# A four-layer transformer kernel with fused expert FFNs: the order of its steps planned by a clock per engine, and the low halves of the weights made by GpSimd

## The chip, the cores and the metric

One NeuronCore of one Trainium2 chip. The metric is the time of one execution on the device in microseconds; the kernel before has a median of 562.09 us in 3 runs.

## The reference

Four layers, all in float32, on `x` of 4 batches x 512 tokens x 128 channels; each layer adds its result to `x`, and reads a layernorm of it:

```python
x = x + attn_a(layernorm(x))    # channel attention, 8 heads of 16 channels, over 512 tokens
x = x + ffn(layernorm(x))       # 8 experts of 336 hidden units, router softmax, actor picks how many
x = x + attn_b(layernorm(x))    # S = q k^T * scale; S *= piecewise factor of sigmoid(S); softmax
x = x + ffn(layernorm(x))       # the same weights again
# ffn: scores = probs where rank(probs) < argmax(actor_logits) + 1
#      out += scores[e] * (silu(h @ gate[e].T) * (h @ up[e].T)) @ down[e].T
```

## The kernel before

The work is cut into steps, each for one batch of 512 tokens. A is the first attention (steps stats, xn, ag, xT, ar, asim, ass, ascale, asT, amax, aexp, awo, am, am2, y), F an FFN (stats, xn, xT, xl, route, rexp, inner, rsum, rrank, tanh, gelu, act, actk, sbc, yT), B the second attention (stats, xn, xT, xl, bqk, bqkl, bs, bsp, bexp, bv, bpT, bo, byx). The F batches 0 to 3 are the first FFN layer, 4 to 7 the second: eight in all.

The FFN's hidden units of all experts stand in 21 chunks (CH) of 128, so there are 168 chunks, numbered k over all eight batches. A chunk is six TensorE passes `gu` (line 1039): gate and up, each as high x high, high x low and low x high in the 4-byte float32r type (`three`, lines 923 to 927); ScalarE's silu of gate into `sl` (616); VectorE's product of up and `sl` into `t2` (`uk`, line 859); GpSimd's product of that with the router's scores `sbc` (`um`, line 513); and the down product into the accumulator bank 7 (line 1061, in float32, two passes). Gate of chunk k waits for silu of k-2, up for the `uk` of k-2. There are 16 buffers `t2`, so gate of chunk k may not be ahead of down of chunk k-16. `um` of a batch needs its `sbc`, so no down product starts before the router chain of its batch (route to sbc) is through.

The weights come from HBM in 21 pieces of 128x384 (192 KB): piece j is gate's (j % 3 = 0), up's (1) or down's (2) of three chunks. ScalarE copies a piece of gate or up to its high half (line 587), VectorE subtracts that from the staged piece to make the low half, WGl or WUl (line 743). Both are parts of the step `wp`, or of `wph` and `wpl` for the first two pieces. TensorE waits before chunks 0, 3, 6, ..., 18 for the low halves of the next three chunks (line 1043).

Every engine runs its part of one list of steps in the order of the list, and waits on semaphores; so the order of the list is the order on each engine. The list comes from `plan()` (line 155). After a written-out PRELUDE it adds for each k the steps `gu` and `uk`, then up to two `um` and `down`, then from each thread (one for each batch of F, A, B, with a start and due offsets in chunks: F_STEPS, A_STEPS, B_STEPS, B_STARTS) the steps that are due at k, and one weight piece at most. A step is put off by one chunk at most if ScalarE's or VectorE's costs of this k exceed TensorE's (COST, DEBT). What was put off in an earlier chunk is otherwise not looked at. B batch 3 starts near chunk 91 and ends with byx behind chunk 131; F batch 7 starts at 132, its sbc stands behind chunk 150.

Matmul results of all steps but the chunks use three PSUM banks in turn (TURNS).

Of the kernel before, what the change touches and what calls it, by code (L numbers as in the profile page):

```python
# [29 lines left out]
F32 = mybir.dt.float32  # L30
# [18 lines left out]
AFTER_POOL = 1.6  # L49
# [42 lines left out]
F_STEPS = [(0, "stats"), (1, "xn"), (3, "xT"), (4, "xl"), (6, "route"), (7, "rexp"), (7, "inner", 0),
           (10, "inner", 1), (9, "rsum"), (12, "rrank"), (12, "tanh"), (12, "gelu"), (14, "act"),
           (14, "actk"), (18, "sbc")]
A_STARTS = (9, 25)
B_STARTS = (25, 48, 67, 90)
M_START = 7
SHIFTS = 1
F_AHEAD = 22


# [7 lines left out]
POOL_COST = dict(um=1.35, stats=1.4, ass=.8, bqkl=1.4, actk=1.1, inner=1)  # L109
COST = dict(stats=(0, 0, 1.2), xn=(0, 0, 1.1), xT=(.4, .5, 0), xl=(0, 0, .6), ag=(.9, .3, 0), ar=(.5, .4, .4),  # L110
            asim=(.7, 0, 0), ass=(0, 0, .1), ascale=(0, 0, .3), asT=(.1, 0, 0), amax=(0, 0, .5), aexp=(0, 3, 0),
            awo=(0, 0, .5), am=(.3, .3, 0), am2=(.3, .3, 0), y=(.9, 0, .6), route=(2, 1.1, .3), rexp=(0, 2.7, 0),
            rsum=(0, 0, 1.3), rrank=(0, 0, 1.1), tanh=(0, .5, 0), gelu=(0, 0, .6), act=(.9, 0, 0), actk=(0, 0, 1.3),
            sbc=(.4, .5, 0), yT=(.4, 0, .6), bqk=(.7, 1, 0), bs=(.7, .5, 0), bsp=(0, 0, .9),
            bv=(.7, 0, .6), bexp=(0, 1.2, 0), bpT=(.4, .5, 0), bo=(.9, .1, 0),
            byx=(0, 0, 1.4))
DEBT = 0.1


def thread(kind, b, steps, start):  # L120

    norm = ("stats", "xn", "xT", "xl")
    return [start, [(s[0], (s[1], kind, b) if s[1] in norm else (s[1], b) + s[2:])
                    for s in steps], 0]


def needs(s):


    kind, b = s[0], s[-1] if s[0] in ("stats", "xn", "xT", "xl") else s[1]  # L130
    prev = b - 1
    if kind == "stats":
        return {"A": [], "F": [("y", b) if b < NB else ("byx", b - NB)], "B": [("yT", b)]}[s[1]]
    if kind == "xT" and s[1] == "A":
        return [("y", b - 2), ("ag", b)]
    if kind == "am2" and b == 0:
        return [("wv", 0)]
    if kind in ("xT", "xl") and s[1] == "B":
        return [("bv", prev)]
    if kind == "bo":  # L140
        return [("bpT", b, i) for i in range(NT)]
    if kind == "yT":
        return [("down", CH * (b + 1) - 1)]
    if kind == "bexp":
        return [("byx", prev), ("bsp", b, s[-1], 3)]
    if kind == "bpT":
        return [("byx", prev)] + [("bexp", b, i) for i in range(NT)]
    return {"ag": [("ar", prev)], "ar": [("asim", prev)], "ass": [("ascale", prev)],
            "ascale": [("asT", prev), ("amax", prev)], "amax": [("aexp", prev)], "aexp": [("am", prev)], "awo": [("am", prev)],
            "am": [("am2", prev)], "am2": [("y", prev)],  # L150
            "bqk": [("bs", prev, NT - 1)], "bs": [("bpT", prev, NT - 1)], "bv": [("byx", prev)],
            "route": [("act", prev)], "rsum": [("actk", prev)], "actk": [("sbc", prev)]}.get(kind, [])


def plan():

    last = CH * 2 * NB
    threads = [thread("F", n, F_STEPS, CH * n - F_AHEAD) if n else thread("F", 0, F0_STEPS, 0) for n in range(2 * NB)]  # L160
    threads += [[CH * (n + 1) + 3, [(0, ("yT", n))], 0] for n in range(2 * NB - 1)]
    threads += [[M_START, [(0, ("wbT", 0)), (2, ("wvp", 0)), (4, ("bvp", 0))], 0]]
    threads += [thread("B", b, B_STEPS, B_STARTS[b]) for b in range(NB)]
    threads += [thread("A", 1, A1_STEPS, 0)] + [thread("A", b, A_STEPS, A_STARTS[b - 2]) for b in range(2, NB)]
    pieces = [("wp", j) for j in range(2, NPIECES)]
    steps, done, order = [], set(), {}
    free_after = []
    debt = [0.0, 0.0]
    pool_free = [0.0]
    um_end, downs = [], [0]  # L170

    def ready(s):
        if not all(v in done or v[1] < 0 for v in needs(s)):
            return False
        if s[0] == "xn" and order[s[1:]] >= 2:
            two_before = [v for v, i in order.items() if i == order[s[1:]] - 2][0]
            if ("xT",) + two_before not in done:
                return False
        if s[0] == "stats" and len(order) >= 2:
            two_before = [v for v, i in order.items() if i == len(order) - 2][0]  # L180
            if ("xn",) + two_before not in done:
                return False
        n = 0 if s[0] == "bo" and s[2] else TURNS.get(s[0], 0)
        return all(len(free_after) + i < 3 or free_after[len(free_after) + i - 3] in done for i in range(n))

    def add(s):
        steps.append(s)
        done.add(s)
        if s[0] in POOL_COST:
            pool_free[0] = max(pool_free[0], k) + POOL_COST[s[0]] / 2.25  # L190
# [12 lines left out]
    def products(k, most):  # L203

        for _ in range(most):
            j = len(um_end)
            if ("uk", j) in done and ("sbc", j // CH) in done and pool_free[0] < k + 1:
                add(("um", j))
                um_end.append(pool_free[0])
            if downs[0] < len(um_end) and um_end[downs[0]] + AFTER_POOL <= k:  # L210
                add(("down", downs[0]))
                downs[0] += 1

    k = -1
    for s in PRELUDE:
        assert ready(s), s
        add(s)
    while k < last - 1:
        if (k + 1) % CH or ("xl", "F", (k + 1) // CH) in done:
            k += 1  # L220
            add(("gu", k))
            assert k < NT2 or ("down", k - NT2) in done
            add(("uk", k))
        else:
            for th in threads:
                th[0] -= th[0] <= k
        products(k, 2)
        pe = 2.2
        act, dve = debt[0] + 0.6, debt[1] + 0.7
        for th in threads:  # L230
            while th[1] and th[0] + th[1][0][0] <= k:
# [5 lines left out]
                if not ready(s) or late:  # L237
                    th[0] += 1
                    th[2] += 1
                    break  # L240
# [936 lines left out]
```

## Time and profile before

| | |
|---|---|
| runs | 560.51, 562.09, 563.34 us; median 562.09 |
| profiled execution | 562.99 us, span 561.2 us, mean granted TensorE clock 0.963 |
| TensorE (PE) busy | 508.4 us, 91% |
| VectorE (DVE) busy | 368.8 us, 66% |
| GpSimd (POOL) busy | 279.2 us, 50% |
| ScalarE (ACT) busy | 239.4 us, 43% |

PE, PEld (its weight loads), DVE, ACT and POOL are the engines' names in the rows. "Busy" counts running instructions; a matmul's end is modelled, so a busy PE can still have short gaps. The granted clock is the share of TensorE's full speed; a stretch at half has 0.5.

### The profile page before, as it was taken

How to read it: one execution, taken by the hardware profiler on the slowest of the kernel's cores; microseconds unless marked ns; L12 is line 12 of the kernel's file. 1: busy time of each engine (PE TensorE's matmuls, PEld its weight loads, DVE VectorE, ACT ScalarE, POOL GpSimd, SP SyncE). 2: the span in 40 equal slices, each digit the busy share in tenths (PEclk: the TensorE clock that was granted, in tenths of full speed). 3: DMA queues.
4: the chain of work that ended last, by engine and by line, in shares of the span. 5: the costliest groups of instructions: out<-in, count | busy, mean ns of one | idle time of the engine just before them, and what ended most of it. 6: DMA issues, size and time to landing. Idle time of an engine off the chain costs nothing. (4 is left out here: it accounts for less than half of the span.)

```text
span 561.2 us, 6465 instructions
## 1 busy us (share of the span) xinstructions
PE 508.4 (91%) x2134; PEld 359.3 (64%) x2134; DVE 368.8 (66%) x781; ACT 239.4 (43%) x399; POOL 279.2 (50%) x268
## 2 busy tenths in 40 slices
PE   7776487999897988999998999979999999999997
PEld 6754364667564764677655677656776576667664
DVE  3646737366649789678989279894797946274221
ACT  3355232444372264732654424744337452433221
POOL 4111516722875239554465434554455455464753
PEclk9979779999998999899998899998999999999999
DMA  8500000000000000000000000000000000000000
GB/s 254 169 1 1 1 0 2 0 0 1 1 2 0 1 0 1 1 0 2 1 1 0 1 0 2 0 0 2 19 2 0 1 19 1 1 2 19 1 0 19
DMA packets 7917, 7.38 MB, mean 13 GB/s; under 512 B 716, under 2 KB 7756, under 8 KB 7884
## 3 DMA queue, kind: packets, MB, share of 16 engines
q1 hardware_dynamic: 7884, 6.97, 4.0%
q8 instruction: 17, 0.28, 0.2%
q14 instruction: 16, 0.13, 0.1%
HBM read 5.91 MB, written 1.05 MB: 12 GB/s over the span
## 5 line engine op out<-in xcount | busy, mean ns | idle before, releaser
L513 POOL TENSOR_TENSOR t<-t,sbc 128x512 f32<-128x512 f32 x168 | 217.5, 1314 | 126.8 <-DVE t L859 98.3
L859 DVE TENSOR_TENSOR t<-bank,sl 128x512 f32<-128x512 f32 x168 | 114.5, 685 | 134.1 <-PE bank L927 106.0
L616 ACT ACTIVATE sl<-bank 128x512 f32<-128x512 f32 x168 | 100.0, 597 | 181.1 <-PE bank L927 163.5
L1061 PE MATMUL bank<-t,WD 128*128 128x512 f32 x336 | 168.2, 603 | 0.0
L925 PE MATMUL bank<-xhF,WGh 128*128 128x512 f32 x168 | 99.6, 593 | 22.4 <-DVE WUl L743 21.2
L1061 PEld LDWEIGHTS bank<-t,WD 128*128 128x128 f32 x336 | 64.7, 192 | 32.6 <-issue 19.8
L925 PE MATMUL bank<-xhF,WUh 128*128 128x512 f32 x168 | 69.1, 411 | 4.1 <-DVE t L859 4.1
L927 PE MATMUL bank<-xhF,WUl 128*128 128x512 f32 x168 | 68.5, 408 | 0.0
L926 PE MATMUL bank<-xlF,WUh 128*128 128x512 f32 x168 | 68.5, 407 | 0.0
L927 PE MATMUL bank<-xhF,WGl 128*128 128x512 f32 x168 | 68.0, 405 | 0.0
L926 PE MATMUL bank<-xlF,WGh 128*128 128x512 f32 x168 | 67.8, 403 | 0.0
L925 PEld LDWEIGHTS bank<-xhF,WGh 128*128 128x128 f32 x168 | 33.0, 196 | 42.6 <-DVE WUl L743 22.8
L718 DVE TENSOR_SCALAR xn<-X,mv,rstd 128x128 f32<-128x128 f32 x64 | 40.3, 691 | 8.8 <-POOL rstd L481 8.8
L926 PEld LDWEIGHTS bank<-xlF,WGh 128*128 128x128 f32 x168 | 33.1, 197 | 17.1 <-issue 15.1
L925 PEld LDWEIGHTS bank<-xhF,WUh 128*128 128x128 f32 x168 | 32.5, 194 | 13.7 <-DVE t L859 6.2
L480 POOL TENSOR_SCALAR rt<-mv 128x4 f32<-128x4 f32 x16 | 3.5, 221 | 73.8 <-DVE mv L707 73.5
L927 PEld LDWEIGHTS bank<-xhF,WUl 128*128 128x128 f32 x168 | 32.7, 195 | 8.3
L927 PEld LDWEIGHTS bank<-xhF,WGl 128*128 128x128 f32 x168 | 32.7, 194 | 7.9
L926 PEld LDWEIGHTS bank<-xlF,WUh 128*128 128x128 f32 x168 | 32.8, 195 | 7.5
L616 ACT ACT_TABLE_LOAD x20 | 25.7, 1283 | 0.4
L500 POOL TENSOR_TENSOR sx<-rk,pr 128x512 f32<-128x512 f32 x8 | 8.4, 1054 | 32.3 <-DVE rk L850 32.3
L646 ACT ACTIVATE Sb<-bank 128x512 f32<-128x512 f32 x16 | 9.6, 599 | 17.7 <-PE bank L927 17.5
(176 smaller groups left out, 683.6 us busy)
## 6 DMA issues: line engine op xcount, KB each, us to landing
stage<-in_gate SPq DMA_DIRECT2D x7, 192.0 KB, 5.3
stage<-in_up SPq DMA_DIRECT2D x7, 192.0 KB, 5.6
WD<-in_down SPq DMA_DIRECT2D x7, 192.0 KB, 5.6
X<-in_x SPq DMA_DIRECT2D x4, 256.0 KB, 5.2
out<-X SPq DMA_DIRECT2D x4, 256.0 KB, 2.3
raw<-in_small SPq DMA_DIRECT2D x1, 388.0 KB, 4.4
raw<-in_small SPq DMA_DIRECT2D x1, 192.0 KB, 2.7
rows<-in_row SPq DMA_DIRECT2D x1, 136.0 KB
```

Source lines behind the costliest of these rows:

```text
L480: chain(pool.tensor_scalar(rt[:, :], mv[:, :, 1], by, more, ALU.mult, ALU.add))
L500: pool.tensor_tensor(sx[:, :, :, :], rk[:, :, :].unsqueeze(3).to_broadcast([P, NT, E, P // E]), pr[:, :, :].unsqueeze(3).to_broadcast([P, ...
L513: pool.tensor_tensor(t2[k % NT2][:, :], t2[k % NT2][:, :], sbc[k // CH % 2][:, :], ALU.mult).then_inc(a_done, 1)
L616: act.activation(sl[k % NSL][:, :], bank[k % 2][:, :], ACT.Silu).then_inc(silu_done, 1)
L646: act.activation(Sb[:, i, :], m_bank(t)[:, :], ACT.Copy).then_inc(n_free(t), 1)
L718: r = dve.tensor_scalar(xn[:, i, :], X[:, NT * q + i, :], mv[:, i, 0:1], rstd[:, i:i + 1], ALU.subtract, ALU.mult)
L859: dve.tensor_tensor(t2[k % NT2][:, :], bank[2 + k % 2][:, :], sl[k % NSL][:, :], ALU.mult).then_inc(t2_done, 1)
L925: pe.matmul(out, lh, rh, start=start, stop=False)
L926: pe.matmul(out, lh, rl, start=False, stop=False)
L927: return pe.matmul(out, ll, rh, start=False, stop=stop)
L1061: pe.matmul(OACC[:, :], WD[:, c, :], t2[k % NT2][:, :], start=(c == 0), stop=(c == CH - 1))\
```

## The change

`plan()` is written anew. It holds a clock for each engine, `t`; STAGES gives for each step the engines it passes through and the time on each; `add` moves the clocks and notes when a step is finished (`fin`). Steps that begin on another engine than TensorE enter when their input is finished and their engine isn't ahead of TensorE by more than DVE_AHEAD, ACT_AHEAD or POOL_AHEAD. Of the steps that begin on TensorE the first ready one in the order of deadlines enters (`threads`, whose first number is the deadline in chunks); then a down product, if its input is finished; else the next chunk; else TensorE's clock goes on by 0.1. `gu` is now two steps, `gate` and `up`, and ScalarE's copy of the accumulator (line 622) is a step of its own, `yc`. Pieces 3 to 20 of the weights (12 of gate and up) have their low half made by GpSimd; two of them are in the prelude.

```diff
-F_AHEAD = 22
+STAGES = dict(
+    stats=(("dve", 1.35), ("pool", 1.5)), xn=(("dve", 1.9),), xT=(("pe", .45), ("act", .6)), xl=(("dve", .7),),
...
+    bexp=(("exp", .85),), bv=(("pe", 1.35), ("dve", .7)), bpT=(("pe", .45), ("act", .6)), bo=(("pe", .9),),
+    byx=(("dve", 2.2),), wp=(("act", .5), ("pool", 1.15)), wph=(("act", .5),), wpl=(("dve", .6),),
...
+TABLE = 1.3
+HOP = 0.1
+PE_MARGIN, BANK_MARGIN = 0.5, 0.3
+DVE_AHEAD, ACT_AHEAD, POOL_AHEAD = 2.6, 1.6, 1.5
+A_FROM = (0, 0, 6, 26)
+F_AHEAD = 24
...
+    threads = [(0, 0, [("wp", j) for j in range(5, NPIECES) if j % 3 != 2])]
+    threads += [(CH * n - 4, CH * n - F_AHEAD, thread("F", n, f_kinds)) for n in range(2 * NB)]
+    threads += [(CH * n - 14, A_FROM[n], thread("A", n, a_kinds)) for n in range(1, NB)]
+    threads += [(CH * (n + 1) + 4, 0, [("yc", n), ("yT", n)]) for n in range(2 * NB - 1)]
+    threads += [(40, 6, [("wbT", 0), ("wvp", 0), ("bvp", 0)])]
+    threads += [(CH * (NB + b) - 12, 0, thread("B", b, b_kinds)) for b in range(NB)]
+    threads.sort(key=lambda th: th[0])
...
+                    if begins <= gus and at <= now + 0.2 and banks_free(s) <= now \
+                            and max(t[e], at) + min(cost, 1.6) <= now + ahead[e]:
+                        add(s)
...
+                if begins <= gus and ready_at(s) + PE_MARGIN <= now and banks_free(s) + BANK_MARGIN <= now:
+                    best = best or (s, th)
...
+        down_at = fin["um", downs] + PE_MARGIN if downs < ums else 1e9
+        if down_at <= now:
+            add(("down", downs))
+            downs += 1
+        elif can_gu and (gu_at <= now + 1.5 or gu_at <= down_at):
+            add(("gate", gus))
+            add(("up", gus))
+            add(("uk", gus))
+            gus += 1
...
+                if kind == "wp":
+                    j = s[1]
+                    pool.wait_ge(wh_ready, 2 * (j // 3) + j % 3 + 1)
+                    hi, lo = piece_of(j)
+                    pool.tensor_tensor(lo, stage[j][:, :], hi.bitcast(F32), ALU.subtract).then_inc(wl_pool, 1)
...
-                if kind in ("wp", "wpl") and s[1] % 3 != 2:
+                if kind == "wpl":
...
-                        pe.wait_ge(wl_dve, 2 * (c // WCH) + 2)
+                        pe.wait_ge(wl_pool if c else wl_dve, 2 * (c // WCH) if c else 2)
```

In these lists of order a row is one instruction of the engine: its place, its line, what it writes and reads; lines of the changed kernel are 62 to 71 higher.

GpSimd, from the norms of the prelude to batch 0's router chain. Before (hq is the router chain's gelu input, sx what sbc is transposed from, t the buffers t2):

```order
40 L480 TENSOR_SCALAR rt_82<-mv_78 128x4
41 L481 TENSOR_TENSOR rstd_80<-rt_82,nhalf 128x4
42 L504 TENSOR_SCALAR hq<-hq 50x512
43 L507 TENSOR_TENSOR hq<-hq,xa 50x512
44 L489 TENSOR_TENSOR rs<-ss,nhalf 128x2
45 L500 TENSOR_TENSOR sx<-rk,pr 128x512
```

The changed kernel, the same place:

```order
43 L574 TENSOR_TENSOR WUl<-stage_141,WUh 128x384
44 L574 TENSOR_TENSOR WGl<-stage_142,WGh 128x384
45 L574 TENSOR_TENSOR WUl<-stage_143,WUh 128x384
46 L551 TENSOR_TENSOR rs<-ss,nhalf 128x2
47 L574 TENSOR_TENSOR WGl<-stage_144,WGh 128x384
48 L574 TENSOR_TENSOR WUl<-stage_145,WUh 128x384
49 L566 TENSOR_SCALAR hq<-hq 50x512
50 L569 TENSOR_TENSOR hq<-hq,xa 50x512
51 L574 TENSOR_TENSOR WGl<-stage_146,WGh 128x384
```

Six weight rests stand ahead of the router chain's first instruction, six behind it, and all twelve ahead of sx.

VectorE, before the actor product of batch 4, which waits for gelu (`hq<-hq,xa`). Before:

```order
356 L859 TENSOR_TENSOR t_118<-bank,sl_102 128x512
357 L824 TENSOR_TENSOR ge<-ge,tri 128x256
358 L826 TENSOR_TENSOR gt<-gt,ge 128x256
359 L827 TENSOR_REDUCE rk<-gt 128x32
360 L832 SCALAR_TENSOR_TENSOR hq<-hq,xa 50x512
361 L893 TENSOR_TENSOR mk_160<-mk_160,mk_162 128x512
```

The changed kernel:

```order
324 L887 TENSOR_TENSOR ge<-pr 128x256
325 L926 TENSOR_TENSOR t_115<-bank,sl_103 128x512
326 L926 TENSOR_TENSOR t_116<-bank,sl_102 128x512
327 L899 SCALAR_TENSOR_TENSOR hq<-hq,xa 50x512
328 L891 TENSOR_TENSOR ge<-ge,tri 128x256
329 L893 TENSOR_TENSOR gt<-gt,ge 128x256
330 L894 TENSOR_REDUCE rk<-gt 128x32
```

The three instructions of rrank have gone behind gelu, and the score instructions on mk that stood among them are elsewhere.

VectorE, where the last B batch ends (byx writes bt and X) and batch 7's norm begins. Before:

```order
558 L908 SCALAR_TENSOR_TENSOR bt<-bank,bri,rows 128x128 x4
559 L912 TENSOR_TENSOR X<-X,bt 128x512
560 L859 TENSOR_TENSOR t_108<-bank,sl_102 128x512
561 L704 BN_STATS bst<-X 128x6 x4
562 L707 BN_AGGR mv_79<-bst 128x2 x4
563 L859 TENSOR_TENSOR t_109<-bank,sl_103 128x512
564 L718 TENSOR_SCALAR xn_76<-X,mv_79,rstd_81 128x128 x4
565 L859 TENSOR_TENSOR t_110<-bank,sl_102 128x512
566 L859 TENSOR_TENSOR t_111<-bank,sl_103 128x512
567 L859 TENSOR_TENSOR t_112<-bank,sl_102 128x512
568 L738 TENSOR_TENSOR xlF_74<-bank,xhF_72 128x512
```

The changed kernel:

```order
560 L975 SCALAR_TENSOR_TENSOR bt<-bank,bri,rows 128x128 x4
561 L979 TENSOR_TENSOR X<-X,bt 128x512
562 L926 TENSOR_TENSOR t_106<-bank,sl_102 128x512
563 L771 BN_STATS bst<-X 128x6 x4
564 L774 BN_AGGR mv_79<-bst 128x2 x4
565 L785 TENSOR_SCALAR xn_76<-X,mv_79,rstd_81 128x128 x4
566 L864 TENSOR_TENSOR X<-bank,X 128x512
567 L805 TENSOR_TENSOR xlF_74<-bank,xhF_72 128x512
568 L926 TENSOR_TENSOR t_107<-bank,sl_103 128x512
```

Before, four products of chunks stand between the norm's first instruction and xlF; now none does: t_106 is chunk 146's and t_107 chunk 147's, which needs xlF. In the changed list batch 7's sbc stands behind chunk 160, with the down product of chunk 147 next. ScalarE's list has 54 table loads (ACT_TABLE_LOAD) instead of 40.

## Rows read from the trace of the kernel before

**Rows 1.** Windows: length; busy us (instructions) of PE, PEld, DVE, ACT, POOL; clock; DMA.
```profile
25.70:94.60 68.90, 46.59 (x186) 34.93 (x186) 40.32 (x87) 28.16 (x52) 22.88 (x21) 0.85 0.00 1
94.60:141.50 46.90, 46.21 (x204) 32.98 (x204) 25.99 (x79) 21.30 (x35) 17.92 (x19) 1.00 0.00 1
141.50:448.40 306.90, 287.68 (x1188) 199.82 (x1188) 242.77 (x456) 145.48 (x233) 168.21 (x140) 0.97 0.01 2
448.40:505.40 57.00, 57.00 (x249) 40.40 (x247) 29.80 (x60) 22.77 (x38) 32.40 (x29) 1.00 0.02 5
```
**Rows 2.** The chain that ended last, near the end: start us, us, what.
```profile
539.50 0.86 PE bank L1061 x2
...
541.75 0.86 PE bank L1061 x2
```
**Rows 3.** Waits of TensorE: waiter <- releaser, us in total, times, longest us.
```profile
PE bank L925 <- DVE WUl L743: 21.2, 6, 7.8
PE bank L945 <- DVE xn L718: 5.3, 5, 2.6
...
PE bank L925 <- DVE xlS L738: 2.9, 1, 2.9
```
**Rows 4.** Timeline from 61 us: start us, us, engine, line, operation.
```profile
61.93 0.53 DVE L743 TENSOR_TENSOR WGl<-stage,WGh 128x384 fp32r<-128x384 f32 x1
...
63.57 8.93 POOL L513 TENSOR_TENSOR t<-t,sbc 128x512 f32<-128x512 f32 x7
63.70 4.87 DVE L718 TENSOR_SCALAR xn<-X,mv,rstd 128x128 f32<-128x128 f32 x4 [0.46 <-POOL rstd L481]
68.50 1.63 DVE L743 TENSOR_TENSOR WUl<-stage,WUh 128x384 fp32r<-128x384 f32 x1
```
**Rows 5.** The chain that ended last, 367 to 379 us.
```profile
367.55 1.51 DVE ge L820
...
370.25 1.47 DVE mk L884
371.72 0.35 DVE mk L885
...
376.25 0.70 DVE hq L832
...
376.99 1.87 PE bank L1029 x8
```
**Rows 6.** Groups by line: busy us, mean ns of one, then idle before.
```profile
L1112 PE MATMUL bank<-v,PT 128*128 128x128 f32 x128 | 15.6, 275 | 0.0
```
**Rows 7.** Groups by line: the low halves on VectorE, the same subtraction on GpSimd.
```profile
L494 POOL TENSOR_TENSOR ql<-qF,qh 128x512 fp32r<-128x512 f32 x4 | 5.6, 1395 | 2.0 <-ACT qh L639 2.0
...
L743 DVE TENSOR_TENSOR WUl<-stage,WUh 128x384 fp32r<-128x384 f32 x7 | 5.4, 775 | 1.9 <-ACT WUh L587 1.8
...
L743 DVE TENSOR_TENSOR WGl<-stage,WGh 128x384 fp32r<-128x384 f32 x7 | 4.0, 574 | 2.2 <-ACT WGh L587 2.2
```
**Rows 8.** Groups by line: GpSimd's products, a table load, the copy of sbc.
```profile
L513 POOL TENSOR_TENSOR t<-t,sbc 128x512 f32<-128x512 f32 x168 | 217.5, 1314 | 126.8 <-DVE t L859 98.3 <-ACT sbc L610 28.1
...
L616 ACT ACT_TABLE_LOAD x20 | 25.7, 1283 | 0.4
...
L610 ACT ACTIVATE sbc<-bank 128x512 f32<-128x512 f32 x8 | 4.8, 597 | 5.0 <-PE bank L1037 5.0
```
**Rows 9.** Timelines of VectorE: batch 0's norm, and byx of B batch 3.
```profile
19.58 0.87 DVE L704 BATCH_NORM_STATS2 bst<-X 128x6 f32<-128x128 f32 x4
...
20.78 1.08 DVE L718 TENSOR_SCALAR xn<-X,mv,rstd 128x128 f32<-128x128 f32 x4
...
24.84 0.69 DVE L738 TENSOR_TENSOR xlF<-bank,xhF 128x512 fp32r<-128x512 f32 x1 [1.38 <-ACT xhF L537]
...
466.14 1.12 DVE L908 SCALAR_TENSOR_TENSOR bt<-bank,bri,rows 128x128 f32<-128x128 f32 x4 [1.09 <-PE bank L1112]
```
**Rows 10.** Groups by line: one of the eight instructions of a score block.
```profile
L884 DVE TENSOR_SCALAR mk<-Sb 128x512 bf16<-128x512 f32 x16 | 11.4, 713 | 6.7 <-ACT Sb L646 6.7
```

More of the change, by code:

```diff
@@ L107 @@
 FREED_BY = dict(asim="ascale", asT="amax", act="actk")
[L109 to L124, printed above, removed]
-def needs(s):
[L130 to L134, printed above, removed]
-        return [("y", b - 2), ("ag", b)]
[L136 to L152, printed above, removed]
@@ L165, in plan @@
-    pieces = [("wp", j) for j in range(2, NPIECES)]
-    steps, done, order = [], set(), {}
-    free_after = []
[L168 to L184, printed above, removed]
+    steps, fin, order = [], {}, {}
@@ L186, in add @@
+    free_after = []
+    t = dict(pe=0.0, act=0.0, dve=0.0, pool=0.0)
+    table = ["exp"]
+    pe_end = {}
     def add(s):
         steps.append(s)
-        done.add(s)
-        if s[0] in POOL_COST:
-            pool_free[0] = max(pool_free[0], k) + POOL_COST[s[0]] / 2.25
+        at = max([fin[v] for v in inputs(s) if v in fin], default=0.0)
+        if s[0] in ("gate", "up"):
+            at = 0.0
+        for e, cost in STAGES[s[0]]:
+            if e in ("exp", "silu"):
+                cost += TABLE * (table[0] != e)
+                table[0] = e
+                e = "act"
+            if s[0] in ("gate", "up") and e == "pe":
+                at = max([fin[v] for v in chunk_inputs(s)], default=0.0)
+            at = max(at + HOP, t[e]) + cost
+            t[e] = at
+            if e == "pe":
+                pe_end[s] = at
+        fin[s] = at
@@ L201, in add, with chunk_inputs @@
             free_after.extend([by] * TURNS[s[0]])
[L203 to L214, printed above, removed]
+    def chunk_inputs(s):
+        k = s[1]
+        n, c = k // CH, k % CH
+        if s[0] == "up":
+            return [("uk", k - 2)] if k >= 2 else []
+        first = [("xl", "F", n)] if c == 0 else []
+        weights = [(w, 3 * (k // WCH) + i) for w in ("wp", "wpl") for i in range(2)] if k < CH and c % WCH == 0 else []
+        return first + [w for w in weights if w in fin] + ([("gate", k - 2)] if k >= 2 else [])
@@ new lines, in banks_free, with ready_at @@
+    def banks_free(s):
+        if s[0] == "bo" and s[2]:
+            return 0.0
+        ends = [free_after[len(free_after) + i - 3] for i in range(TURNS.get(s[0], 0)) if len(free_after) + i >= 3]
+        return max([fin.get(v, 1e9) for v in ends], default=0.0)
+    def ready_at(s):
+        before = [s[:1 + (s[0] in ("stats", "xn", "xT", "xl"))] + (batch(s) - 1,) + s[2 + (s[0] in ("stats", "xn", "xT", "xl")):]]
+        if s[0] == "wp":
+            before = []
+        if not all(v in fin or batch(v) < 0 for v in inputs(s) + needs(s) + before):
+            return 1e9
+        if s[0] == "xn":
+            i = order[s[1:]]
+            others = [v for v, j in order.items() if j == i - 1]
+            two = [v for v, j in order.items() if j == i - 2]
+            if not all(("xn",) + v in fin for v in others) or not all(("xT",) + v in fin for v in two):
+                return 1e9
+        if s[0] == "stats":
+            two = [v for v, j in order.items() if j == len(order) - 2]
+            if not all(("xn",) + v in fin for v in two):
+                return 1e9
+        return max([fin[v] for v in inputs(s)], default=0.0)
@@ L215, in plan @@
     for s in PRELUDE:
-        assert ready(s), s
+        assert ready_at(s) < 1e8 and banks_free(s) < 1e8, s
         add(s)
[L218 to L223, printed above, removed]
-        else:
[L225 to L231, printed above, removed]
-                s = th[1][0][1]
-                cost = COST.get(s[0], (0, 0, 0))
-                room = pe + cost[0] + DEBT
-                late = (th[2] < SHIFTS
-                        and (act + cost[1] > room + (cost[1] > 2) * 3 or dve + cost[2] > room))
[L237 to L240, printed above, removed]
-                th[1].pop(0)
-                add(s)
-                pe, act, dve = pe + cost[0], act + cost[1], dve + cost[2]
-        if pieces:
-            add(pieces.pop(0))
-        debt = [max(0.0, act - pe), max(0.0, dve - pe)]
@@ L247, in plan @@
-    assert not any(th[1] for th in threads)
-    while downs[0] < last:
-        k += 1
-        products(k, 2)
+    norm = ("stats", "xn", "xT", "xl")
+    f_kinds = [(k,) for k in norm] + [("route",), ("rexp",), ("inner", 0), ("inner", 1), ("rsum",), ("tanh",), ("gelu",),
+                                      ("rrank",), ("act",), ("actk",), ("sbc",)]
+    a_kinds = [(k,) for k in ("stats", "xn", "ag", "xT", "ar", "asim", "ass", "ascale", "asT", "amax", "aexp", "awo",
+                              "am", "am2", "y")]
@@ new lines, in plan, with thread @@
+    b_kinds = [("stats",), ("xn",), ("xT",), ("xl",), ("bqk", 0), ("bqkl", 0), ("bqk", 1), ("bqkl", 1)]
+    for i in range(NT):
+        b_kinds += [("bs", i)] + [("bsp", i, part) for part in range(4)] + [("bexp", i)] + [("bv",)] * (i == 0)
+    b_kinds += [("bpT", j) for j in range(NT)] + [("bo", i) for i in range(NT)] + [("byx",)]
+    def thread(what, b, kinds):
+        all_ = [(k[0], what, b) if k[0] in norm else (k[0], b) + k[1:] for k in kinds]
+        return [s for s in all_ if s not in fin]
@@ new lines, in plan @@
+    threads.sort(key=lambda th: th[0])
+    gus, ums, downs = 0, 0, 0
+    ahead = dict(dve=DVE_AHEAD, act=ACT_AHEAD, pool=POOL_AHEAD)
+    while downs < last:
+        now = t["pe"]
+        more = True
+        while more:
+            more = False
+            for _, begins, th in threads:
+                for s in [v for v in th if STAGES[v[0]][0][0] != "pe"]:
+                    e, cost = STAGES[s[0]][0]
+                    e = "act" if e == "exp" else e
+                    at = ready_at(s)
+                    if begins <= gus and at <= now + 0.2 and banks_free(s) <= now \
+                            and max(t[e], at) + min(cost, 1.6) <= now + ahead[e]:
+                        add(s)
+                        th.remove(s)
+                        more = True
+            if ums < gus and ("sbc", ums // CH) in fin and fin["uk", ums] <= now + 0.2 and t["pool"] <= now + 0.4:
+                add(("um", ums))
+                ums += 1
+                more = True
+        best = None
+        for _, begins, th in threads:
+            for s in [v for v in th if STAGES[v[0]][0][0] == "pe"]:
+                if begins <= gus and ready_at(s) + PE_MARGIN <= now and banks_free(s) + BANK_MARGIN <= now:
+                    best = best or (s, th)
+        if best:
+            add(best[0])
+            best[1].remove(best[0])
+            continue
+        first = [v for v in [("xl", "F", gus // CH)] if gus % CH == 0]
+        weights = [("wp", 3 * (gus // WCH) + i) for i in range(2)] if 2 * WCH > gus >= CH or WCH <= gus < CH else []
+        can_gu = gus < last and all(v in fin for v in first + weights) and (gus < NT2 or downs > gus - NT2)
+        gu_at = max([fin[v] for v in chunk_inputs(("gate", gus)) + chunk_inputs(("up", gus))], default=0.0) if can_gu else 1e9
+        down_at = fin["um", downs] + PE_MARGIN if downs < ums else 1e9
[7 more added lines that the diff above has]
+            gus += 1
+        elif down_at < 1e8:
+            add(("down", downs))
+            downs += 1
+        else:
+            t["pe"] += 0.1
+            assert t["pe"] < 2000, [th for th in threads if th[2]][:3]
@@ L251, in plan @@
+    while any(th for _, _, th in threads):
+        for _, _, th in threads:
+            while th and ready_at(th[0]) < 1e8:
+                add(th.pop(0))
+    add(("yc", 2 * NB - 1))
     add(("yT", 2 * NB - 1))
```

97 lines of the change are left out of this document (63 added, 34 removed).

## The prediction

> **What bounds the kernel now.** I read the busy times by stage first, then who waits for whom on TensorE, then the chain and two short timelines. Bounds of the stages: the gate and up products of a chunk are numbered 0 to 167; chunk 0 starts at 25.7 us, chunk 18 at 94.6, chunk 35 at 141.5, chunk 126 at 448.4. TensorE is the engine to fill: of the four stages shown two have it busy all the time [rows 1]. The stage 25.7 to 94.6 has 68.90 us and 46.59 busy, so 22.3 idle, at a mean granted clock of 0.85; at half clock (1.2 instead of 2.4 GHz) busy time is twice what it need be, so another 0.15 x 68.9 = 10.3 us is lost, 32.6 in all. The stage 141.5 to 448.4 loses 306.90 - 287.68 = 19.2 idle and 0.03 x 306.9 = 9.2 to the clock: 28.4. The two stages 94.6 to 141.5 and 448.4 to 505.4 lose under 1 us. Even running, a chunk of six gate/up passes and one down product takes 2.25 us, of which the down is 0.86, so gate and up take 1.39 [rows 2].
>
> Who ends TensorE's waits [rows 3]: the largest is the low half of the weights, made by VectorE (WUl, line 743), 21.2 us in 6 waits. The timeline shows one of them: the second piece stands on VectorE behind four xn instructions that take 4.87 us, because each has to take turns with a GpSimd product t, and then needs 1.63 us itself [rows 4]; this is TensorE's longest wait, 7.8 us [rows 3]. The WGl piece just ahead, with GpSimd quiet, takes 0.53 us [rows 4]. In the long stage the chain goes through VectorE: ge, mk, gt and rk run before hq (gelu), and only then may the actor product L1029 start [rows 5].
>
> The busy times understate the long stage, since the modelled ends of matmuls cover part of each restart. By pace it holds 91 gate/up pairs (126.5 us), 101 downs (86.9) and some 55 us of other products (an estimate: the products of four B batches and five router chains, of whose rows by line L1112's 15.6 us is the largest [rows 6]). That is 268 us in 306.9, so about 38 lost. I use 38, with 28.4 as the low end.
>
> **The change, part by part.** All sums start from the profiled execution, 563.0 us (its span is 561.2); the median of the runs is 562.1, 0.9 less.
>
> *Weight rests to GpSimd, and earlier (chunks 0 to 17).* 12 of the 14 rests leave VectorE and stand on GpSimd, most of them ahead of chunk 8, while GpSimd is busy 22.9 of 68.9 us [rows 1]. VectorE needs 574 ns for one of gate's and 775 for one of up's; GpSimd has no row of 128x384, but the same subtraction of 128x512 takes 1395 ns there [rows 7], so about 1.05 us for three quarters of it (bounds 0.57 and 1.4). 12 x 1.05 = 12.6 us of GpSimd, beside matmuls. If the cover were gone, a late pair would cost 2.1 us. ScalarE makes the high halves earlier too, 12 x 0.5 us moved, none added. What is late next: (a) the products of batch 0 now begin only after chunk 15, because the router's weights (sbc) come after it, and the first down waits for ScalarE's copy, 0.6, and a GpSimd product, 1.31 [rows 8], with hops 2.3 us, nothing between on TensorE; (b) without downs between them two chunks last 2.8 us, and each excursion to the exponential needs two table loads of 1.28 [rows 8]: two of them stall TensorE by about 2 us each, 4; (c) one contended xn, 2; (d) clock, 2 (before, 22.3 idle brought 10.3). 10.3 of 32.6 stay: **22 saved** (bounds 14 and 28).
>
> The Trainium skill's GPSIMD Engine Reference (side-by-side cycle accounting of elementwise work) holds that two-input elementwise work runs about twice as fast on VectorE and belongs there; the durations above agree with its ratio. By that rule the move costs 12 x 0.5 = 6 us of engine time; the sum counts none of it, because GpSimd has the room and TensorE doesn't wait for it.
>
> *Order by due time (chunks 18 to 146).* rrank goes behind gelu, so the actor product no longer waits for gt, ge and rk; parts of B's scores stand singly between the uk products; products that need xl or hq enter after other work. Before, TensorE lost 38 here. What stays: contended xn, today 5.3 + 2.9 in waits [rows 3], 8; the half clock, reduced with the stalls, 4; the first down of a batch now often stands right behind the last of the batch before and waits for ScalarE's copy of the accumulator (0.6 and hops, four places), 3; and 54 table loads instead of 40 (bexp goes in singly, with silu between): 14 x 1.28 = 18 us of ScalarE, which is busy 145 of 307 us, of which I let 3 reach TensorE. Bounds of the last: 0 and 18. 18 of 38 stay: **20 saved** (bounds 3 and 30; the low end takes 28.4 lost and 25 staying). Nothing else is added to VectorE: it is busy 242.8 us in a stage that holds 268 of matmul [rows 1], so TensorE stays the bound, if narrowly.
>
> *The end (chunk 147 on).* The last B batch is drawn out to chunk 145, and batch 7's norm starts behind it. Before, it was at chunk 132 and cost nothing: the stage 448.4 to 505.4 has no idle time at all [rows 1]. Now stats, rstd, xn, transposes, xh and xl stand between byx and chunk 147. With empty queues that took from 19.58 to 25.53 us less 1.1 for another xn, 4.9 [rows 9]; byx adds 1.12 [rows 9], the write to X behind it about 0.7 (as one product t) and hops. Some 7 us, under which lie chunk 146 (1.39), a down (0.86) and yT (0.44): 4.3 idle, 5 with the uk that stands between. Then sbc of batch 7 comes after chunk 160 instead of 150, with d147 right behind it: 2.3 idle. After it 21 GpSimd products of 1.31 are 27.6 us, beside 7 x 1.39 + 21 x 0.86 = 27.8 of matmul, so GpSimd and TensorE end together and one down is left over: 1. Clock after the stalls: 2. **10 lost** (bounds 6 and 18; the cover of 14 chunks without downs, 19.5 us, for the router chain is thin: were it 5 short, they would be added).
>
> The prelude and DMA: two high halves move into the prelude on ScalarE between copies it waits for anyway, SP's order is unchanged. 0.
>
> Sum: 563.0 - 22 - 20 + 10 = 531, rounded to **532**.
>
> **The rivals.**
> *A, nearly all waits go.* If the order hides xn and the tables too, 8 stay in the middle instead of 18, and 7 of 32.6 in the first stage: 563 - 26 - 30 + 9 = 516. For it: before, the stages without B batches run gapless. Against: VectorE's load. 0.17.
>
> *B, GpSimd and VectorE shut each other out.* GpSimd's products and VectorE's SBUF instructions shut each other out: xn 4.87 [rows 4] instead of 1.08 [rows 9], the WUl piece 1.63 instead of 0.53 [rows 4]. Then rests on GpSimd hold up VectorE for up to 12.6 us where they relieve it, and bursts of products after each sbc catch xn of the next norm three more times at 3 us. Savings: 22 - 6 = 16 and 20 - 9 = 11, and 11 lost: 547. For it: in [rows 4] it is just such a burst. Against: most rests come before the first product. 0.15. The Trainium skill's SBUF — State Buffer (two separate sides) has this as an exclusive lock of the port pair that both engines share, held for a whole instruction; the trace agrees, each xn there lasting about one product of 1.3 us.
>
> *C, slower: VectorE becomes the pace.* Each of the 16 score blocks has eight instructions on mk and Sb alone, 128 in all, and each can wait for one product of GpSimd. [Rows 5] has L884 at 1.47 us, its neighbours at 0.35 to 0.42 ran free; the mean of L884 is 713 ns [rows 10]. If their mean rises by 0.45 us, VectorE's 243 us in the middle become 300, more than 268 of matmul, and with the two in step to nine tenths the stage takes 332 instead of 307: 563 - 22 + 25 + 10 = 576. It decides from a mean of about 1.1 us for these. 0.07.
>
> *D, nothing gained:* stalls change places, their sum stays (563, 0.05): new waits of 32 us would have to be found.
>
> **How the numbers follow.** My forecast, 520 to 542, has 0.56; A 0.17; B 0.15; C 0.07; D 0.05. The range for 8 in 10 leaves out C, D and the fast end of A, and keeps B: 511 to 552. Half a per cent, 2.8 us, is about what a measurement can tell here. Faster by more than that: forecast, A and B, 0.88. Within it: most of D, 0.04. Slower: C and the rest of D, 0.08.
>
> **What would show it.** Right: no wait of TensorE for the low half of a weight over 1 us; chunk 18 starts near 73 us; idle time of TensorE in the middle about halved; an idle stretch of 4 to 6 us before chunk 147, one of about 2 us before the first down of batch 7. Wrong: TensorE waiting long for rests made by GpSimd (first term); TensorE's waits for VectorE's t as long as before or VectorE busy above nine tenths of the middle (second term); GpSimd ending well after TensorE's last gate/up pair has been covered, or the router chain of batch 7 not done by chunk 160 (third term).

## The result, and the profile after

The changed kernel takes 604.64 us (median of 4 runs, 603.51 to 607.97), the kernel before 562.72 in the same comparison: ratio 1.0744, 95% interval 1.0666 to 1.0822. Forecast were 532 us and a range of 511 to 552. The sign was wrong. Times given for the runs below are medians of all their runs, but for link_uk, the only one of them whose runs fall in two groups (586.1 and 586.5 us, and 595.8 twice at a lower granted clock): its time is that of the faster two, its profile is of a slower one.

The windows of the profile after, at the same chunks as [rows 1] (chunk 0 starts at 25.8 us, 18 at 71.1, 126 at 454.0, 147 at 542.3; the middle is cut at chunks 35 and 84):

```profile
25.80:71.10 45.30, 41.32 (x192) 31.23 (x191) 28.98 (x79) 27.01 (x50) 25.32 (x26) 0.96 0.00 1
71.10:138.40 67.30, 64.02 (x272) 42.97 (x273) 47.04 (x109) 28.87 (x49) 46.77 (x43) 1.00 0.00 1
138.40:305.00 166.60, 146.64 (x571) 96.87 (x569) 112.16 (x214) 79.57 (x120) 81.19 (x68) 0.97 0.00 1
305.00:454.00 149.00, 130.51 (x542) 88.55 (x541) 95.08 (x179) 66.87 (x101) 66.05 (x55) 0.98 0.01 2
454.00:542.30 88.30, 66.19 (x243) 42.56 (x241) 41.93 (x77) 30.56 (x46) 31.77 (x25) 0.89 0.02 5
542.30:606.20 63.90, 56.38 (x195) 37.38 (x195) 19.48 (x41) 18.22 (x29) 29.00 (x24) 0.93 0.02 6
```

Chunks 0 to 17 take 45.3 us instead of 68.9 [rows 1], 23.6 less. Chunks 18 to 125 take 382.9 (71.1 to 454.0) instead of 353.8 (94.6 to 448.4), 29.1 more. Chunks 126 to 146 take 88.3 instead of 57.0 [rows 1], 31.3 more, and the rest 63.9 instead of 55.8, 8.1 more. That sums to 44.9; the spans (606.2 and 561.2) differ by 45.0. VectorE is not the pace: where the time is lost it is busy 112 of 167 us and 95 of 149 (before, 243 of 307), then 42 of 88 (before, 30 of 57).

TensorE's waits, by total, answer to [rows 3]:

```profile
PE bank L1132 <- POOL t L580: 46.9, 33, 4.9
PE bank L1012 <- DVE xn L785: 10.8, 6, 2.6
PE bank L992 <- ACT sl L683: 4.6, 6, 1.2
PE bank L1048 <- DVE simT L836: 2.7, 2, 1.9
PE bank L1132 <- ACT YT L689: 2.3, 3, 0.8
```

The 21.2 us for WUl are gone. In their place stand 46.9 us in 33 waits of a kind that the list of TensorE's waits in the kernel before has not at all: the down product (L1132) waits for GpSimd's product t (L580). The weight loads ahead of it wait 74.0 us for the same. GpSimd itself isn't late from work; it waits for VectorE's product, and that for up:

```profile
POOL t L580 <- DVE t L926: 143.1, 59, 5.9
DVE t L926 <- PE bank L994: 142.3, 71, 6.0
```

The timeline at chunk 142 shows one round trip from start to end (weight loads left out; L1171 is a transpose of the second attention):

```profile
510.47 0.40 PE L994 MATMUL bank<-xhF,WUl 128*128 128x512 f32 x1
510.71 0.60 PE L1171 MATMUL bank<-ident,Sb 128*128 128x128 f32 x4
510.91 0.69 DVE L926 TENSOR_TENSOR t<-bank,sl 128x512 f32<-128x512 f32 x1 [5.94 <-PE bank L994]
...
511.68 1.26 POOL L580 TENSOR_TENSOR t<-t,sbc 128x512 f32<-128x512 f32 x1 [5.38 <-DVE t L926]
513.00 1.13 PE L1132 MATMUL bank<-t,WD 128*128 128x512 f32 x2 [1.69 <-POOL t L580]
```

The chunk's own down product stands right behind its up and one transpose. From the end of up the product on VectorE, then the one on GpSimd take 2.1 us, and TensorE stands 1.69. VectorE had been idle 5.94 and GpSimd 5.38. Nothing is too slow here; the order asks for the product too soon.

### The profile page after: what moved, and what is told of

It is laid out like the page before. It is cut to its first block and busy times, and to the rows that moved or that the text cites. A ratio compares the mean times of both kernels' runs of the same rounds, so it can differ in the third digit from the quotient of the medians.

```text
span 606.2 us, 6477 instructions
## 1 busy us (share of the span) xinstructions
PE 524.6 (87%) x2134; PEld 357.0 (59%) x2134; DVE 357.0 (59%) x769; ACT 259.2 (43%) x413; POOL 291.2 (48%) x280
## 5 line engine op out<-in xcount | busy, mean ns | idle before, releaser
L580 POOL TENSOR_TENSOR t<-t,sbc 128x512 f32<-128x512 f32 x168 | 218.4, 1323 | 152.6 <-DVE t L926 143.1
L1132 PE MATMUL bank<-t,WD 128*128 128x512 f32 x336 | 176.2, 634 | 49.5 <-POOL t L580 46.9
L1132 PEld LDWEIGHTS bank<-t,WD 128*128 128x128 f32 x336 | 59.9, 196 | 105.6 <-POOL t L580 74.0
L992 PE MATMUL bank<-xhF,WGh 128*128 128x512 f32 x168 | 97.4, 580 | 6.0 <-ACT sl L683 4.6
L993 PEld LDWEIGHTS bank<-xlF,WGh 128*128 128x128 f32 x168 | 32.9, 196 | 19.0 <-issue 15.7
L992 PEld LDWEIGHTS bank<-xhF,WUh 128*128 128x128 f32 x168 | 32.3, 192 | 10.7 <-DVE t L926 3.2
L785 DVE TENSOR_SCALAR xn<-X,mv,rstd 128x128 f32<-128x128 f32 x64 | 35.1, 610 | 3.6 <-POOL rstd L543 3.5
L725 ACT ACTIVATE PT<-bank 128x512 f32<-128x512 f32 x16 | 9.6, 598 | 28.8 <-PE bank L1171 28.8
```

What stands on the lines that cost most here:

```text
L580: pool.tensor_tensor(t2[k % NT2][:, :], t2[k % NT2][:, :], sbc[k // CH % 2][:, :], ALU.mult).then_inc(a_done, 1)
L725: act.activation(PT[:, j, :], m_bank(t)[:, :], ACT.Copy).then_inc(n_free(t), 1)
L785: r = dve.tensor_scalar(xn[:, i, :], X[:, NT * q + i, :], mv[:, i, 0:1], rstd[:, i:i + 1], ALU.subtract, ALU.mult)
L992: pe.matmul(out, lh, rh, start=start, stop=False)
L993: pe.matmul(out, lh, rl, start=False, stop=False)
L1132: pe.matmul(OACC[:, :], WD[:, c, :], t2[k % NT2][:, :], start=(c == 0), stop=(c == CH - 1))\
```

## Why: the planner's clock lacks links

`inputs(s)` gives what a step must wait for in the planner's clock. It has entries for the steps of A, B and F, but none for uk, um and down, so they fall to an empty list. A uk then "ends" 0.7 us after VectorE's clock is free, be it before its own up product; a um ends 1.35 us after GpSimd's clock is free. For chunk 142 the planner's clock has the up product end at 434.3, its uk at 428.7 and its um at 430.6, so the down product counts as due at once. Where VectorE and GpSimd have a backlog, their clocks stand later than TensorE's and hold the products back by themselves, and the error is small. Where they have room, it is up to the whole round trip.

A count from the lists: down products with under 2.4 us of TensorE work, by the planner's own costs, between their chunk's up and themselves. The kernel before has 0, since its planner keeps a down AFTER_POOL = 1.6 chunks behind its um; the changed kernel has 27, of which 16 in batches 5 and 6. Below, a down under this limit is called near. I call this theory L (the links missing in the planner). Its rivals: T, the 14 more table loads; V, VectorE's load or order in the middle.

## The experiments

All were run beside the kernel before (560.8 to 562.1 us median, by comparison). A ratio is the run's time over that of the kernel before, with its 95% interval.

**One part alone: the rests on GpSimd, old order** (the old step wp, its VectorE part moved to GpSimd).

```diff
-                if kind in ("wp", "wpl") and s[1] % 3 != 2:
+                if kind == "wpl":
...
+                if kind == "wp" and s[1] % 3 != 2:
+                    j = s[1]
+                    pool.wait_ge(wh_ready, 2 * (j // 3) + j % 3 + 1)
...
```

> The kernel before with one part of the change: the low halves of pieces 3 to 20 are made by GpSimd, in the old order. My first term (the VectorE waits for WUl cost 22 us, most of which go): 541 to 553 us, and no wait of TensorE over 1 us for a low half. The rule against elementwise work on GpSimd, or the two engines shutting each other out: 558 or more, with new waits of TensorE for WUl on GpSimd.

559.42 us, ratio 0.9939 (0.9904 to 0.9975). A miss: 3 us instead of 9 to 21. TensorE's first wait in the profile:

```profile
PE bank L930 <- POOL WUl L512: 18.9, 6, 4.2
```

The wait is nearly what it was in [rows 3] (21.2 in 6), with another name. The engine was not its main cause.

**Holding the down products back.** The changed kernel's list, then one pass that moves down products alone. It lets one go early only where the next gate or the batch's yc needs it (`must`): two near downs stay, chunks 146 and 167.

```diff
+def hold(steps):
...
+    out, held, work, seen = [], [], 0.0, {}
+    for s in steps:
+        if s[0] == "down":
+            held.append(s[1])
+            continue
+        if s[0] == "yc":
+            must = CH * (s[1] + 1) - 1
+        elif s[0] == "gate":
+            must = s[1] - NT2
...
+        while held and seen[held[0]] + HOLD <= work:
+            out.append(("down", held.pop(0)))
+            work += 0.86
...
```

> The changed kernel, its list as planned, but each down product is moved back behind at least 2.4 us of other TensorE work after its chunk's up product and its um. Theory L (links missing: in the planner's clock uk doesn't wait for gate and up, um not for uk, so 27 downs stand too close behind their chunk, and TensorE waits 46.9 us for GpSimd's t): 560 to 580 us, that wait under 20 us. Rival T (54 table loads instead of 40, single bexp steps) or rival V (VectorE paces the middle): over 595, the wait for t only changes its name.

566.41 us, ratio 1.0060 (1.0024 to 1.0096); as expected of L, and 38 below the changed kernel, by moving nothing but down products. The 54 table loads and VectorE's order are the same, so T and V are out as main causes.

```profile
PE bank L1162 <- POOL t L610: 11.3, 11, 4.6
PE bank L1042 <- DVE xn L815: 9.8, 6, 3.0
```

> The changed kernel with each down product held behind 1.0 us of other TensorE work instead of 2.4: 18 downs under 2.4 us, 27 without. Theory L, by dose: between the changed kernel (604) and hold_2p4 (566), 580 to 597.

574.80 us, ratio 1.0257 (1.0175 to 1.0339): between the two as L has it, but 5 us below the range that I gave, a miss in size. The wait for t is 22.1 us. So by dose 604.6, 574.8, 566.4 us with waits for t of 46.9, 22.1, 11.3.

> As hold_2p4 with 3.8 us. Theory L: 553 to 572, the wait for t under 12 us, a little better than 2.4 as VectorE and GpSimd queues are covered too. Rivals T and V: over 595.

580.07 us, ratio 1.0288 (1.0216 to 1.0361): a miss. The wait for t fell to 8.3, but the one for xn rose from 9.8 to 16.6, and the stretches of the profile at half the granted clock from 30 to 55 us. Why products held this long meet xn more often I didn't settle.

**The links put in.**

```diff
+            "uk": lambda: [("gate", b), ("up", b)],
+            "um": lambda: [("uk", b), ("sbc", b // CH)],
+            "down": lambda: [("um", b)] + ([("yc", b // CH - 1)] if b % CH == 0 and b else []),
...
-                    dve.reciprocal(bri[:, :], brs[:, :])
+                    chain(dve.reciprocal(bri[:, :], brs[:, :]))
```

The last line gives one VectorE instruction a wait for itself, which the new order needs.

> The changed kernel with the missing links put into the planner's inputs: uk needs gate and up of its chunk, um needs uk and sbc, a batch's first down needs yc; one VectorE instruction (bri) gets a wait for itself, which the new order needs. Theory L: the waits for t at downs under 10 us, and 535 to 575 in all; the new clock shows chunks running out before batches 5, 6 and 7, 20 us or so of TensorE idle before chunks 105, 126 and 147, which may take part of the gain. Rivals T and V: over 590, since tables (52) and VectorE's work are the same.

573.35 us, ratio 1.0185 (1.0118 to 1.0252). In the range, and the gain is there, 31 us; the wait for t is 11.6, just over the 10 of the expectation. One near down is left. It is still 7 us slower than hold_2p4: the stop between up of chunk 146 and chunk 147 is longer (25.4 us; 10.7 in hold_2p4, 11.1 in the changed kernel), and so are chunks 0 to 17 (see the table below).

> The changed kernel with one link alone: um waits in the planner's clock for uk (and sbc), uk still for nothing. 6 downs under 2.4 us instead of 27. Theory L: 565 to 585, waits for t 15 to 30 us, since uk's end is still set too early where VectorE is idle. Otherwise 600 or more.

568.16 us, ratio 1.0100 (1.0052 to 1.0149); the wait for t is 15.6 us.

> The changed kernel with the other link alone: uk waits for gate and up, um for nothing; 15 downs under 2.4 us. Theory L: between link_um and the changed kernel, 575 to 598. If only the number of table loads or VectorE's load counted: as the changed kernel, 600 or more.

586.3 us, ratio 1.0437 (1.0386 to 1.0488); the wait for t is 23.1 us in its profile. One link alone goes with the counts: 27 near downs take 604.6 us, 15 take 586.3, 6 take 568.2. Both links leave one near down and take 573.4, more than the um link alone, with a longer stop before chunk 147 (25.4 us instead of 15.4). So the count does not decide the time by itself.

**The illness given to the old kernel.**

```diff
-AFTER_POOL = 1.6
+AFTER_POOL = 0.0
```

> The kernel before with AFTER_POOL 0 instead of 1.6, nothing else: its planner no longer keeps a down product 1.6 chunks behind its um, and 47 downs then have under 2.4 us of TensorE work since their chunk's up product (0 before, 27 in the changed kernel). Theory L: the same illness in the old kernel, waits of TensorE for GpSimd's t of 35 us or more and 590 to 625 us. If nearness of downs is not the cause: within 6 us of before.

582.64 us, ratio 1.0371 (1.0336 to 1.0406). One number of the old planner makes it 22 us slower, with the same wait (other steps move a little with it: byx of the last B batch stands behind chunk 128 instead of 131):

```profile
PE bank L1061 <- POOL t L513: 22.0, 23, 2.6
PE bank L925 <- DVE WUl L743: 20.9, 6, 7.5
```

The size was overrated, a miss on both counts: 22 us of waits, where I expected 35, and 582.6 instead of 590 or more. 47 near downs cost 22 us, in the changed kernel 27 cost 38. The lists show what the count leaves out, how near they are. Here 46 of the 47 have 2.26 us of work ahead of them, and all together lack 8 us of their 2.4 each. In the changed kernel 13 of the 27 have under 1 us, and together they lack 32; in hold_1p0 it is 15, in hold_2p4 3. The waits for t go with this sum better than with the count (46.9, 22.1 and 11.3 us), but not in proportion: here 8 us lacking cost 22 of waits.

**Table loads.** B's exponentials in pairs, 50 loads for 54.

> The changed kernel with the softmax exponentials of B in pairs as before (50 table loads instead of 54). Rival T (tables cost): 5 us or more below the changed kernel, 599 or less. Theory L (downs too near their chunks, 29 of them here, 27 there): within 5 us of it, 600 to 610, the wait for GpSimd's t at downs as long as before, 40 us or more.

611.22 us, ratio 1.0884 (1.0812 to 1.0955). The wait for t was 49.2 us, and the gain that T asks for did not come. The 7 us more are just outside the expectation. But this order has nearer downs too (29, which lack 42 us), so the run gives no price for a table load; against T the stronger case is hold_2p4, which keeps all 54.

**Place or engine of the weight rests.** In the old planner, two pieces for each chunk:

```diff
-    pieces = [("wp", j) for j in range(2, NPIECES)]
+    pieces = [("wp", j) for j in range(2, NPIECES) if j % 3 != 2]
...
-        if pieces:
-            add(pieces.pop(0))
+        for _ in range(2):
+            if pieces:
+                add(pieces.pop(0))
```

> The kernel before, the twelve gate and up pieces two per chunk from chunk 0 on (down pieces, which need no step, taken out of the list); low halves still on VectorE. Rests_alone gained 3 us, and TensorE still waited 18.9 us for low halves from GpSimd. If the late place in the list is the cause (theory P): 540 to 552 us, waits for low halves under 8 us. If the engine is (theory E, my first term as written): 556 or more.

544.63 us, ratio 0.9685 (0.9618 to 0.9752).

> As old_early_dve, with the low halves on GpSimd. Theory P: within 4 us of old_early_dve. Theory E: 10 us or more below it.

549.20 us, ratio 0.9761 (0.9697 to 0.9824). Theory P, the place. In old_early_dve no wait for WUl is left among the longest; its first rows are

```profile
PE bank L926 <- DVE t L860: 6.0, 6, 1.9
PE bank L988 <- issue: 5.9, 3, 2.9
```

With the rests on GpSimd it is 4.6 us slower (546.2 to 550.1 against 544.0 to 546.0; no run overlaps), just past the 4 that I allowed. Part of that is clock: at the same mean granted clock, 0.981, the run with GpSimd took 546.2 and those with VectorE 544.0 to 545.0.

> The changed kernel with the weight rests back on VectorE, in the same early places (cost in the planner moved to VectorE too). Theory P: 600 to 612, chunk 18 starts near 75 us, no long wait for low halves. Theory E: 615 or more.

610.08 us, ratio 1.0853 (1.0789 to 1.0916), where the changed kernel has 1.0744 (1.0666 to 1.0822): P again, and TensorE has no wait for a low half in its list. The longest are for t, 45.7 us. Here GpSimd is the faster maker: no run overlaps (609.4 to 610.7 with VectorE, 603.5 to 608.0 with GpSimd), and chunks 0 to 17 take 49.4 us instead of 45.3; but the intervals of the two ratios do overlap.

**gelu ahead of rrank alone**, in old_early_dve:

```diff
-           (10, "inner", 1), (9, "rsum"), (12, "rrank"), (12, "tanh"), (12, "gelu"), (14, "act"),
+           (10, "inner", 1), (9, "rsum"), (12, "tanh"), (12, "gelu"), (12, "rrank"), (14, "act"),
```

> old_early_dve (the old order with the weight pieces two per chunk, 544.6 us) with rrank behind tanh and gelu in F_STEPS. My second term: the actor product L1029 waited for gt, ge and rk ahead of gelu; this alone should give 4 to 10 us, 535 to 541. If VectorE's load is what it waits for, and not the order: within 2 us of old_early_dve.

545.43 us, ratio 0.9712 (0.9674 to 0.9750); old_early_dve has 544.63. Nothing gained, a miss of my 4 to 10. The wait of L1030 for hq, 4.3 us in old_early_dve, is gone from the list, and the one of up for VectorE's t is 8.9 instead of 6.0:

```profile
PE bank L926 <- DVE t L860: 8.9, 9, 1.9
PE bank L946 <- DVE xn L719: 5.3, 5, 2.6
PE bank L959 <- DVE xn L719: 4.0, 3, 2.6
```

**The late end of B, and what is best.**

```diff
-DVE_AHEAD, ACT_AHEAD, POOL_AHEAD = 2.6, 1.6, 1.5
+DVE_AHEAD, ACT_AHEAD, POOL_AHEAD = 5.0, 3.0, 2.0
```

> hold_2p4 with DVE_AHEAD, ACT_AHEAD, POOL_AHEAD 5.0, 3.0, 2.0 instead of 2.6, 1.6, 1.5: VectorE's steps enter earlier, byx of the last B batch stands behind chunk 137 instead of 145 and batch 7's sbc behind 151 instead of 160. If the late end of B is what still keeps hold_2p4 (566) over old_early_dve (545): 540 to 555. If it is something else (tables, spread-out scores): 560 or more.

562.94 us, ratio 1.0018 (0.9985 to 1.0051): a miss, 3.5 us below hold_2p4. In the profiled runs chunk 126 starts at 442.5 us with 119 to the end; in hold_2p4 it starts at 427.3 with 135 to the end. So the last part gained 17 us. There the 10.7 us between up of chunk 146 and chunk 147 in hold_2p4 are gone, as byx now ends sooner. But the three numbers move steps everywhere, so how much of the 17 is the end of B alone is not shown. Ahead of chunk 126 they cost 15 us, 5 more busy and 10 more idle on TensorE. Chunks 0 to 17 have 228 matmuls instead of 192, from later chunks, and are 15.7 us longer; chunks 18 to 125 don't get shorter for it. The waits for VectorE's t and for silu grew (3.5 and 2.4 us in hold_2p4):

```profile
PE bank L1042 <- DVE xn L815: 12.8, 7, 2.8
PE bank L1022 <- DVE t L956: 9.8, 9, 2.4
PE bank L1022 <- ACT sl L713: 6.6, 7, 1.6
PE bank L1162 <- POOL t L610: 3.8, 3, 1.7
```

> links (573) with the same three numbers 5.0, 3.0, 2.0; byx of B batch 3 stays behind 145, batches 4 and 5 get their sbc at 83 and 108 instead of 94 and 120. Theory of the late B: the middle gains, the end doesn't: 550 to 565.

543.64 us (538.12 to 544.25), ratio 0.9656 (0.9584 to 0.9727), again outside the range, on the good side: with the links in place the further look ahead pays, 30 us below links. From up of chunk 146 to chunk 147 it takes 9.3 us instead of 25.4, and the middle is shorter too (see the table below). Why it costs hold_2p4 its first part and not this kernel was not tried.

```profile
PE bank L1015 <- DVE xn L788: 7.1, 5, 3.7
PE bank L995 <- ACT sl L686: 5.9, 9, 1.2
PE bank L1135 <- POOL t L583: 5.6, 5, 4.1
PE bank L995 <- DVE t L929: 4.2, 6, 1.2
```

This and old_early_dve beat both kernels, by 3.4% and 3.2% on the one before; between the two the intervals don't decide.

Where the time goes, in the profiled runs (us):

| | chunks 0 to 17 | 18 to 125 | 126 to 146 | 147 to the end |
|---|---|---|---|---|
| before | 68.9 | 353.8 | 57.0 | 55.8 |
| changed | 45.3 | 382.9 | 88.3 | 63.9 |
| hold_2p4 | 42.0 | 359.8 | 73.0 | 62.4 |
| hold_2p4_ahead | 57.7 | 359.1 | 60.3 | 58.5 |
| links | 50.7 | 354.1 | 76.8 | 62.9 |
| links_ahead | 40.7 | 346.6 | 66.9 | 60.9 |
| old_early_dve | 53.7 | 350.9 | 57.9 | 55.8 |

## The prediction, step by step

- **First term, 22 us saved: right in size, in part by luck.** Chunks 0 to 17 lost 23.6 us, chunk 18 started at 71.1 (73 forecast), and no wait for a low half was left. But I put the rests' engine first ("12 of the 14 rests leave VectorE"). In the old order the engine alone gave 3 us, the earlier place alone 16, 15 of them in these chunks, and the engine on top of the place cost 5. The other 8 of the 23.6 came with the new order; 4 of them go with GpSimd there (new_dve_rests). What stays was put at 10.3; it is 4.0 idle and 1.8 of clock, 5.8.
- **Second term, 20 saved in chunks 18 to 146: this step failed.** The windows have 471.2 us there instead of 410.8, 60.4 more. My list of what stays (18 of 38: xn 8, clock 4, ScalarE's copy 3, tables 3) has no entry for down products that wait for GpSimd's t. That term was put at nothing without a reason; it measured 42.4 us in this stretch, of the 46.9 in all. I weighed what the planner's costs are, and never asked what a down product's due time is worked out from. The list held the answer: 27 downs stand under 2.4 us of work behind their chunk. The price was in the trace before, too: on average 0.69 us for the product t and 1.31 for GpSimd's, end to end. Holding the downs back takes 38.4 of the 60.4 away (432.8 us).
- **The gain itself was not there either.** "The actor product no longer waits for gt, ge and rk" was true, and worth nothing (old_early_gelu). All of TensorE's waits for gelu in the kernel before were short:

```profile
PE bank L1029 <- DVE hq L832: 4.3, 3, 1.7
```

  With the near downs gone this stretch is still 22 us longer than before (hold_2p4), with the best list 2.7 longer (413.5, links_ahead). No run saved the 20 us. The stop before chunk 147 is 9 of the 22; for the rest no run names one cause. The xn that I put at 8, from "5.3 + 2.9", is a misreading, since the 2.9 in [rows 3] is a wait for xlS; TensorE's waits for xn are 12.2 us in the changed kernel.
- **My rivals.** A took away more of the waits, B and C asked whether GpSimd and VectorE would be in each other's way or too busy, and D named no cause. The loss came where both were idle. Rival C forecast 576 by VectorE's pace, and VectorE was busy two thirds of the middle. None of them went up to 604.6.
- **Third term, 10 lost from chunk 147 on: a little small, inside its bounds.** The part behind chunk 147 took 8.1 us more. Behind up of chunk 146 I expected 4.3 us idle, or 5. These are the rows:

```profile
530.85 0.39 PE L994 MATMUL bank<-xhF,WUl 128*128 128x512 f32 x1
536.19 2.08 PE L1132 MATMUL bank<-t,WD 128*128 128x512 f32 x2 [4.95 <-POOL t L580]
538.96 1.11 PE L1140 MATMUL bank<-ident,YT 128*128 128x128 f32 x4 [0.69 <-ACT YT L689]
539.87 1.06 PE L1012 MATMUL bank<-ident,xn 128*128 128x128 f32 x4
542.34 0.79 PE L992 MATMUL bank<-xhF,WGh 128*128 128x512 f32 x1 [1.41 <-DVE xlF L805]
542.93 0.63 PE L993 MATMUL bank<-xlF,WGh 128*128 128x512 f32 x1
```

  That is 11.1 us from the end of up to chunk 147, 7.05 idle and 4.05 busy, where the kernel before has 1.8. With the 8.1 it makes some 17 us, at the upper bound of 18. The down product that I had counted as cover waited itself, its um standing on GpSimd behind the norm's rstd. The matmuls behind run at half clock (0.63 instead of 0.40 us).
- **Sum by these parts:** 23.6 saved, 17.4 lost at the end, and 51.1 in the middle (the 60.4 without the 9.3 that chunk 147 waits longer), so 44.9 lost in all. The terms of the prediction sum to 531; the 532 is a slip of 1 us that changes nothing.
- **Table loads, 3 us:** no run here shows a price for them.
- **Clock:** 2 for the end; the last window has 0.07 x 63.9 = 4.5 us. The one before it, which had a clock of 1.00 in the kernel before, has 0.11 x 88.3 = 9.7.

## What to carry to other kernels

Where a planner orders the work, check its clock for every kind of step before its costs: a step without inputs counts as due too early, and worst where the engines have room. Count in the finished list how much work stands between each consumer and what it consumes, and price the round trip from the trace. And when a late result is moved to another engine, ask first whether it merely stands too late in the list.

## What was unexpected of the hardware

Which engine makes the twelve low halves counted for little, and not always the same way: with GpSimd instead of VectorE 559.4 against 562.1 us in the old places, 549.2 against 544.6 early in the old order, 604.6 against 610.1 in the new one. And yet one of them takes GpSimd 1.03 to 1.11 us (changed kernel) and VectorE 0.57 to 0.70 (old_early_dve).

TensorE's clock made the losses at the end dearer: from 454 us on the changed kernel's granted clock is 0.89, then 0.93, where the kernel before had 1.00 and 0.99. Its longest stretch at half clock, 17 us from 533.4 to 550.5, begins inside the idle time behind chunk 146: the engine had last run at 531.2, and stood until 536.2. Over the whole kernel the stretches at half clock sum to 51 us, in the kernel before to 44, about half of it in chunks 0 to 17.
